# Expert rows of a fused attention and mixture-of-experts kernel: TensorE transposes replaced by DMA transposes of fp16 halves

## The chip, the cores and the metric

The kernel runs on one core of a Trainium2 chip. The metric is the device time of one execution in microseconds (us); lower is better. Names used below: PE is TensorE's matmul, PEld its weight load, DVE is VectorE, ACT is ScalarE, POOL is GpSimd, SP is the sync engine, which here only starts DMAs.

## The reference

Input x is 8 sequences of 512 tokens with 256 features, fp32: 4096 tokens. Each token is normalised (xn). Two branches read xn.

- A recurrent branch: q = xn Wq, v = xn Wv, a scan along the sequence (state = lam * state + v, one lam for each of 16 heads), y = q * state, layer norm of y with gain and bias, times silu(xn Wg), times Wo.
- A mixture of 8 experts, 2 for each token, with softmax gates of the two largest router logits. Its core is

```
def expert_step(acc, ew):
    wi, wo, g = ew
    h = x @ wi.T                      # 256 -> 2 x 512
    a, b = jnp.split(h, 2, axis=-1)
    o = jax.nn.silu(a) * b @ wo.T     # 512 -> 256
    return (acc + g[:, None] * o, None)
```

The output is x + s * silu(moe + bias), where s is the first branch.

## The kernel before, in words

All matmuls use fp16 operands with a high and a low half: a product is the sum of three matmuls (high by high, high by low, low by high), which the helper `three` issues (L1091).

First part, up to about 158 us: normalisation, routing, the recurrent branch chunk by chunk (8 chunks of 512 tokens), conversion of the expert weights to fp16 halves, and the sorting of tokens by expert. The sorting is done by GpSimd with 64 indirect DMAs (L462) that write each normalised row with four more columns (expert, two gate values, token number) to `slots_dram`, 260 words a row.

Second part, the expert blocks. 32 pair blocks (`PAIRS`) of 256 rows and 7 single blocks (`SINGLES`) of 128 rows. Block b uses buffer b % 2 of each kind. For a block:

- SP loads its rows from `slots_dram` to `slot_in` (`load_slots`, L346 to L353; the register with the row number is read with a small load from SBUF first). It waits until the buffer's last transposes are done (`slot_t_ps`) and until GpSimd has read the four extra columns of block b - 2 (`meta_ready`).
- PE transposes the fp32 rows to PSUM (`transpose_slots`, L1215: 4 instructions for a pair block, 2 for a single one), ACT copies them to fp16 (`high_slots`, L672), DVE writes the low half (`low_slots`, L995). Both land in `xT`, the moving operand of the first matmuls.
- PE computes `hidden(b, 0)` in bankA and `hidden(b, 1)` in bankB (24 matmuls each), ACT and DVE make silu(a) * b and its fp16 halves (L680, L1001, L685, L1005), and PE computes `outputs(b - 1)` in bankC (24 matmuls). The order on PE in the loop is hidden(b, 0), transposes of b + 1, hidden(b, 1), outputs(b - 1).
- DVE scales the result by the gate (L1020, `gate_y`), and GpSimd adds the rows to `y_dram` with two indirect DMAs (L532, `scatter_y`), each block after the scatters of the block before have landed. Then it works on the four extra columns of the next block (`meta`, L486 to L498, whose last instruction raises `meta_ready`).

Single blocks run with the roles of the operands exchanged (`row_hidden`, `transpose_g`). While early blocks run, SP also loads x for the last stage (L365, blocks 2 to 8) and the extra columns of the single blocks (L370, behind block 9).

Third part: `y_dram` comes back, silu, product with s, sum with x, store.

The order of work on each engine is written out by hand. Semaphores alone tie the engines together.

Of the kernel before, what the change touches and what calls it, by code (L numbers as in the profile page):

```python
# [33 lines left out]
P = 128  # L34
# [54 lines left out]
def scatters_before(b, i):  # L89

    if not isinstance(b, int):
        return b if i == 0 else b - 1
    return sum(units(a) for a in range(i, b, 2))

# [8 lines left out]
def build(nc, x, wq, wv, wg, wo, beta, ln_g, ln_b, router, w_exp, bias, out):  # L103
    ctx = ExitStack()
    with ctx:
# [52 lines left out]
        slot_in = [part(rows_raw, SB * ROW).rearrange("p (s r) -> p s r", r=ROW) for _ in range(2)]  # L158
# [83 lines left out]
        slots_ps = [bankD[:, i, :].rearrange("p (k n) -> p k n", k=KD) for i in range(2)]  # L242
# [9 lines left out]

        first_slots_ps = [bankB[:, i, :].rearrange("p (k n) -> p k n", k=KD) for i in range(2)]

        def slots_ps_of(b, i):
            return first_slots_ps[i] if isinstance(b, int) and b < 2 else slots_ps[i]

# [25 lines left out]
        slot_t_ps, slot_hi_ready, slot_lo_ready, h_ps, y_ps, y_sb = map(  # L283
            sem, ("slot_t_ps", "slot_hi_ready", "slot_lo_ready", "h_ps", "y_ps", "y_sb"))
# [21 lines left out]
        def _(sp):  # L306
# [39 lines left out]
            def load_slots(b, i):  # L346
                if not isinstance(b, int) or b >= 2:
                    sp.wait_ge(slot_t_ps, b - 1)
                if not isinstance(b, int) or 2 <= b < PAIRS + 2:
                    sp.wait_ge(meta_ready, b - 1)  # L350
                row = sp.value_load(blk_row[0:1, bass.ds(b, 1)], min_val=0, max_val=E * REGION // P)
                sp.dma_start(slot_in[i][:, 0:units(b), :], slots_v[:, bass.ds(row, units(b)), :])\
                  .then_inc(slot_loaded[i], 16)  # L353

            def two(b):
                load_slots(b, 0)
                load_slots(b + 1, 1)
# [14 lines left out]
            repeat(sp, X_EARLY + 3, PAIRS, 2, two)  # L372
            for b in range(PAIRS, BLOCKS):
                load_slots(b, b % 2)
# [5 lines left out]
            for i in range(2):  # L380
                sp.wait_ge(y_scattered[i], 16 * scatters_before(BLOCKS, i))
# [14 lines left out]
        def _(pool):  # L396
# [83 lines left out]
            def meta(b, i, first):  # L480

                pool.wait_ge(slot_loaded[i], b * 8 + 16 if i == 0 else b * 8 + 8)
# [3 lines left out]
                pool.tensor_tensor(is_first[i][:, :], slot_in[i][:, :, D], e_b, ALU.subtract)\  # L486
# [7 lines left out]
                pool.tensor_tensor(gate_c[i][:, :], slot_in[i][:, :, D + 1], is_first[i][:, :], ALU.mult)\  # L494
                    .then_inc(pool_step, 1)
                pool.wait_ge(pool_step, b * 3 + n_meta + 3)
                pool.tensor_tensor(gate_c[i][:, :], gate_c[i][:, :], slot_in[i][:, :, D + 2], ALU.add)
                pool.tensor_copy(dest_f[i][:, :], slot_in[i][:, :, D + 3]).then_inc(meta_ready, 1)  # L498
# [15 lines left out]
            def scatter_y(b, i, first=False):  # L514
# [7 lines left out]
                if not ones:  # L522
                    pool.wait_ge(meta_ready, b + 1)
                    if not isinstance(b, int) or b >= 2:
                        pool.wait_ge(y_scattered[i], 16 * scatters_before(b, i))
# [34 lines left out]
        def _(act):  # L560
# [78 lines left out]
            def recur(c, convert=True, last=False):  # L639
# [10 lines left out]
                if last:  # L650
                    act.wait_ge(rows_scattered, 16 * N_SCATTERS)
                    high_slots(0, 0, True)
                    high_slots(1, 1, True)
# [11 lines left out]
            def high_slots(b, i, first):  # L665
                act.wait_ge(slot_t_ps, b + 1)
                if isinstance(b, int) and b >= PAIRS + 2:
                    act.wait_ge(one_h_ps, b - PAIRS - 1)
                elif not first:
                    act.wait_ge(h_ps, b * 2 - 2)  # L670
                n = units(b) * P
                act.activation(xT[i][:, 0:KD, 0:n], slots_ps_of(b, i)[:, :, 0:n], ACT.Copy)\  # L672
# [15 lines left out]
            def halves(b, i, before, last=False):  # L688
                half(b, i, 0, before)
                if not last:  # L690
                    high_slots(b + 1, 1 - i, before == 0)
# [8 lines left out]
            split_p(CH)  # L700
            half(1, 1, 0, 1)
            keep_s(CH)
            high_slots(2, 0, False)
# [7 lines left out]
            for n in range(SINGLES):  # L711
# [7 lines left out]
                if n < SINGLES - 1:  # L719
                    high_slots(b + 1, 1 - i, False)  # L720
# [15 lines left out]
        def _(dve):  # L736
# [255 lines left out]
            def low_slots(b, i):  # L992
                dve.wait_ge(slot_hi_ready, b + 1)
                n = units(b) * P
                dve.tensor_tensor(xT[i][:, KD:2 * KD, 0:n], slots_ps_of(b, i)[:, :, 0:n],  # L995
                                  xT[i][:, 0:KD, 0:n], ALU.subtract).then_inc(slot_lo_ready, 1)
# [11 lines left out]
            def gate_y(b, i, first):  # L1008
# [6 lines left out]
                if not first:  # L1015

                    dve.wait_ge(y_scattered[i], 16 * scatters_before(b, i))
# [6 lines left out]
            def halves(b, i, last=False):  # L1024
                half(b, i, 0)
                if not last:
                    low_slots(b + 1, 1 - i)
# [7 lines left out]
            low_p(CH)  # L1035
            halves(1, 1)
# [10 lines left out]
            for n in range(SINGLES):  # L1047
# [6 lines left out]
                if n < SINGLES - 1:  # L1054
                    low_slots(b + 1, 1 - i)
# [30 lines left out]
        def _(pe):  # L1086
# [122 lines left out]
            def transpose_slots(b, i, first):  # L1209
                pe.wait_ge(slot_loaded[i], b * 8 + 16 if i == 0 else b * 8 + 8)  # L1210
                if not first:
                    pe.wait_ge(slot_lo_ready, b - 1)
                for k in range(KD):
                    for s in range(units(b)):
                        last = pe.transpose(slots_ps_of(b, i)[:, k, s * P:s * P + P],  # L1215
# [138 lines left out]
```

## Time and profile before

| | us |
|---|---|
| median of 3 runs | 508.69 (508.16 to 510.36) |
| the profiled execution, its own time | 510.48 |
| its span (first to last instruction) | 508.7 |
| PE busy | 425.2 (84%) |
| DVE busy | 304.3 (60%) |
| POOL busy | 275.1 (54%) |
| ACT busy | 214.3 (42%) |

The span is what the profiler recorded between the first and the last instruction; the execution's own time is 1.8 us longer. A share of busy time is an average over three parts with different limits, so the rows below are taken stage by stage.

### The profile page before, as it was taken

How to read it: one execution, taken by the hardware profiler on the slowest of the kernel's cores; microseconds unless marked ns; L12 is line 12 of the kernel's file. 1: busy time of each engine (PE TensorE's matmuls, PEld its weight loads, DVE VectorE, ACT ScalarE, POOL GpSimd, SP SyncE). 2: the span in 40 equal slices, each digit the busy share in tenths (PEclk: the TensorE clock that was granted, in tenths of full speed). 3: DMA queues.
4: the chain of work that ended last, by engine and by line, in shares of the span. 5: the costliest groups of instructions: out<-in, count | busy, mean ns of one | idle time of the engine just before them, and what ended most of it. 6: DMA issues, size and time to landing. Idle time of an engine off the chain costs nothing.

```text
span 508.7 us, 12049 instructions
## 1 busy us (share of the span) xinstructions
PE 425.2 (84%) x3446; PEld 337.6 (66%) x3447; DVE 304.3 (60%) x602; ACT 214.3 (42%) x340; POOL 275.1 (54%) x504
## 2 busy tenths in 40 slices
PE   1758784998898899999999989999999999998000
PEld 1544452565557798887898878888888888765000
DVE  4898899999965545454454544454545454444055
ACT  4882372778756534342324233333333333232041
POOL 4626786688772046564646474556565646543232
PEclk9999898999999999999999999999999999999755
DMA  8992275566933226455343433343334333342499
GB/s 250 290 362 94 84 244 190 164 240 242 329 121 84 82 46 144 106 101 104 54 73 52 73 53 50 64 67 62 58 66 69 61 56 59 65 64 32 73 310 349
DMA packets 52692, 64.70 MB, mean 127 GB/s; under 512 B 5552, under 2 KB 47536, under 8 KB 52656
## 3 DMA queue, kind: packets, MB, share of 16 engines
q1 hardware_dynamic: 37712, 45.55, 28.9%
q0 software_dynamic: 13296, 17.83, 20.8%
q10 hardware_dynamic: 1664, 1.06, 0.7%
q8 instruction: 10, 0.16, 0.1%
q14 instruction: 10, 0.08, 0.0%
HBM read 40.02 MB, written 28.74 MB: 135 GB/s over the span
## 4 chain that ended last, share of the span: by engine, by line
PE 40%; DMA 18%; issue 14%; DVE 13%; POOL 8%; ACT 3%; SPq 2%; DVEq 1%; POOLq 0%; ACTq 0%
PE bankC L1091 14%; PE bankB L1091 12%; DMA y_dram<-rows_raw 11%; PE bankA L1091 9%; POOL slots_dram L462 4%; DMA rows_raw<-slots_dram 4%; PE bankD L1215 2%; DMA w_raw<-x_in 2%; DVE rows_raw L1020 2%; POOL stat L426 1%; DVE w_raw L935 1%; DVE work L926 1%; DMA w_raw<-y_dram 1%; POOL y_dram L532 1%; DVE bn L751 1%
## 5 line engine op out<-in xcount | busy, mean ns | idle before, releaser
L532 POOL DMA_INDIRECT y_dram<-rows_raw x71 | 113.2, 1595 | 49.3 <-issue 31.0
L1091 PE MATMUL bankC<-w_raw,rows_raw 128*128 x852 | 99.5, 273 | 1.7 <-DVE rows_raw L1058 1.6
L1091 PEld LDWEIGHTS bankC<-w_raw,rows_raw 128*128 128x128 f16 x852 | 82.1, 98 | 13.3 <-issue 2.5
L462 POOL DMA_INDIRECT slots_dram<-rows_raw,pos_i x64 | 74.1, 1157 | 30.8 <-issue 20.0
L1091 PE MATMUL bankA<-rows_raw,w_raw 128*128 128x256 f16 x768 | 89.1, 273 | 1.2 <-DVE rows_raw L995 1.2
L1091 PE MATMUL bankB<-rows_raw,w_raw 128*128 128x256 f16 x768 | 89.1, 273 | 0.0
L1091 PEld LDWEIGHTS bankA<-rows_raw,w_raw 128*128 x768 | 75.0, 98 | 10.1 <-issue 1.4
L1091 PEld LDWEIGHTS bankB<-rows_raw,w_raw 128*128 x768 | 75.1, 98 | 8.3
L1005 DVE TENSOR_TENSOR rows_raw<-rows_raw 128x512 f16<-128x512 f32 x64 | 44.3, 692 | 45.7 <-ACT rows_raw L685 45.7
L1001 DVE SCALAR_TENSOR_TENSOR rows_raw<-rows_raw,bankA 128x512 f32<-128x512 f32 x32 | 22.0, 687 | 73.6 <-ACT rows_raw L680 73.6
L680 ACT ACTIVATE rows_raw<-bankA 128x512 f32<-128x512 f32 x32 | 19.1, 597 | 101.1 <-PE bankA L1091 101.1
L685 ACT ACTIVATE rows_raw<-rows_raw 128x512 f16<-128x512 f32 x64 | 40.3, 630 | 49.6 <-DVE rows_raw L1001 49.6
L526 POOL TENSOR_TENSOR spare<-spare 128x1 f32<-128x1 f32 x32 | 6.2, 192 | 95.7 <-DVE rows_raw L1020 94.7
L1020 DVE TENSOR_SCALAR rows_raw<-bankC,rows_raw 128x256 f32<-128x256 f32 x71 | 31.4, 480 | 9.6 <-DMA y_dram<-rows_raw 7.5
L1001 DVE SCALAR_TENSOR_TENSOR rows_raw<-rows_raw,bankB 128x512 f32<-128x512 f32 x32 | 22.0, 687 | 15.9 <-ACT rows_raw L680 15.9
L680 ACT ACTIVATE rows_raw<-bankB 128x512 f32<-128x512 f32 x32 | 19.1, 597 | 22.3 <-PE bankB L1091 22.3
L935 DVE SCALAR_TENSOR_TENSOR w_raw<-work,w_raw 128x1024 f32 (+1 forms) x24 | 27.7, 1215 | 0.0
L995 DVE TENSOR_TENSOR rows_raw<-bankD,rows_raw 128x512 f16<-128x512 f32 (+1 forms) x37 | 23.4, 633 | 2.4 <-ACT rows_raw L672 2.4
L1215 PE MATMUL bankD<-ident,rows_raw 128*128 128x128 f32 x134 | 21.4, 278 | 3.6 <-DMA rows_raw<-slots_dram 3.3
L426 POOL TENSOR_TENSOR stat<-stat,neg_half 128x4 f32<-128x4 f32 x16 | 16.9, 1058 | 13.0 <-DVE stat L964 12.2
L486 POOL TENSOR_TENSOR rows_raw<-rows_raw,blk_e 128x2 f32<-128x2 f32 x32 | 23.8, 743 | 0.0
L1091 PE MATMUL bankC<-wat_hi,work 128*128 128x256 f16 x128 | 22.3, 273 | 1.8 <-DVE work L980 1.4
(190 smaller groups left out, 641.2 us busy)
## 6 DMA issues: line engine op xcount, KB each, us to landing
work<-w_exp_in SPq DMA_DIRECT2D x24, 512.0 KB, 5.2
rows_raw<-slots_dram SPq DMA_DIRECT2D x32, 260.0 KB, 2.8
w_raw<-x_in SPq DMA_DIRECT2D x9, 512.0 KB, 4.4
y_dram<-bias_in SPq DMA_DIRECT2D x4, 1024.0 KB, 12.5
w_raw<-y_dram SPq DMA_DIRECT2D x8, 512.0 KB, 7.7
out<-w_raw SPq DMA_DIRECT2D x8, 512.0 KB, 5.7
work<-x_in SPq DMA_DIRECT2D x7, 512.0 KB, 4.4
slots_dram<-fill SPq DMA_DIRECT2D x9, 260.0 KB, 5.2
```

The costliest lines, as they stand in the source:

```text
L462: pool.indirect_dma_start(out=slots_dram, out_offset=bass.IndirectOffsetOnAxis(slot, 0), in_=row, in_offset=None, bounds_check=SLOTS - 1, ...
L486: pool.tensor_tensor(is_first[i][:, :], slot_in[i][:, :, D], e_b, ALU.subtract)\
L532: pool.indirect_dma_start(out=y_dram, out_offset=bass.IndirectOffsetOnAxis(to, 0), in_=ys[i][:, s, :], in_offset=None, bounds_check=ROWS_O ...
L680: act.activation(sil[j][:, :, 0:n], AB[j][:, :, 0:n], ACT.Silu, scale=1.0 / WSCALE).then_inc(sil_ready, 1)
L685: act.activation(g_hi[i][:, 2 * j:2 * j + 2, 0:n], g32[j][:, :, 0:n], ACT.Copy)\
L935: dve.scalar_tensor_tensor(w_lo[:, piece], wst[:, i % STAGES, :], WSCALE, w_hi[:, piece], ALU.mult, ALU.subtract).then_inc(w_lo_ready, 1)
L995: dve.tensor_tensor(xT[i][:, KD:2 * KD, 0:n], slots_ps_of(b, i)[:, :, 0:n], xT[i][:, 0:KD, 0:n], ALU.subtract).then_inc(slot_lo_ready, 1)
L1001: dve.scalar_tensor_tensor(g32[j][:, :, 0:n], sil[j][:, :, 0:n], 1.0 / WSCALE, AB[j][:, :, BLOCK:BLOCK + n], ALU.mult, ALU.mult).then_inc( ...
L1005: dve.tensor_tensor(g_lo[i][:, 2 * j:2 * j + 2, 0:n], g32[j][:, :, 0:n], g_hi[i][:, 2 * j:2 * j + 2, 0:n], ALU.subtract).then_inc(g_split, 1)
L1020: last = dve.tensor_scalar(ys[i][:, s, :], bankC[:, i, s * D:s * D + D], gates[:, s:s + 1], None, ALU.mult)
L1091: last = pe.matmul(out_ap, lhsT, rhs, start=(n == 0), stop=(n == len(todo) - 1))
L1215: last = pe.transpose(slots_ps_of(b, i)[:, k, s * P:s * P + P], slot_in[i][:, s, k * P:k * P + P], ident32[:, :])
```

## The change

- The rows of a block are loaded without the four extra columns (256 words instead of 260) to `slot_in`. The four columns are loaded by a DMA of their own to `meta_in` (`load_meta`), for the 32 pair blocks.
- ACT casts the rows to fp16 from SBUF, in the row layout, to the high half of `split16`, and DVE writes the low half beside it. The transposes on PE are gone. SP transposes the 128 x 512 fp16 values of each 128 rows with one DMA from SBUF to SBUF (`dma_start_transpose`), two for a pair block, one for a single block, 71 in all.
- ACT and DVE do this for block b + 2 between the two halves of block b (before: for block b + 1).
- SP's order for a block: load the extra columns of b (waits for `meta_ready` of b - 2); wait for `slot_lo_ready` of b and for both hidden halves of b - 2; load the rows of b + 2; transpose block b.
- PE waits for `xt_loaded` ahead of hidden(b, 0).

The core of the diff:

```diff
@@ SP @@
             def load_slots(b, i):
-                if not isinstance(b, int) or b >= 2:
-                    sp.wait_ge(slot_t_ps, b - 1)
-                if not isinstance(b, int) or 2 <= b < PAIRS + 2:
-                    sp.wait_ge(meta_ready, b - 1)
                 row = sp.value_load(blk_row[0:1, bass.ds(b, 1)], min_val=0, max_val=E * REGION // P)
-                sp.dma_start(slot_in[i][:, 0:units(b), :], slots_v[:, bass.ds(row, units(b)), :])\
+                sp.dma_start(slot_in[i][:, 0:units(b), :], slots_v[:, bass.ds(row, units(b)), 0:D])\
                   .then_inc(slot_loaded[i], 16)
+            def load_meta(b, i):
+                if not isinstance(b, int) or b >= 2:
+                    sp.wait_ge(meta_ready, b - 1)
+                row = sp.value_load(blk_row[0:1, bass.ds(b, 1)], min_val=0, max_val=E * REGION // P)
+                sp.dma_start(meta_in[i], slots_v[:, bass.ds(row, SB), D:ROW]).then_inc(meta_loaded[i], 16)
+            def transpose_slots(b, i):
+                sp.wait_ge(slot_lo_ready, b + 1)
+                if isinstance(b, int) and b >= PAIRS + 2:
+                    sp.wait_ge(one_h_ps, b - PAIRS - 1)
+                elif not isinstance(b, int) or b >= 2:
+                    sp.wait_ge(h_ps, b * 2 - 2)
+                if not isinstance(b, int) or b + 2 < BLOCKS:
+                    load_slots(b + 2, i)
+                for s in range(units(b)):
+                    sp.dma_start_transpose(xT[i][:, :, s * P:s * P + P],
+                                           split16[i][:, s, :, :].rearrange("p h d -> p (h d)"))\
+                      .then_inc(xt_loaded[i], 16)
+            for b in range(2):
+                load_slots(b, b)
+            for b in range(2):
+                load_meta(b, b)
+            for b in range(2):
+                transpose_slots(b, b)
...
@@ GpSimd, meta(b, i, first) @@
-                pool.wait_ge(slot_loaded[i], b * 8 + 16 if i == 0 else b * 8 + 8)
+                pool.wait_ge(meta_loaded[i], b * 8 + 16 if i == 0 else b * 8 + 8)
...
@@ ACT @@
-            def high_slots(b, i, first):
-                act.wait_ge(slot_t_ps, b + 1)
...
-                act.activation(xT[i][:, 0:KD, 0:n], slots_ps_of(b, i)[:, :, 0:n], ACT.Copy)\
+            def high_slots(b, i):
+                act.wait_ge(slot_loaded[i], b * 8 + 16 if i == 0 else b * 8 + 8)
+                if not isinstance(b, int) or b >= 2:
+                    act.wait_ge(xt_loaded[i], 16 * units_before(b, i))
+                act.activation(split16[i][:, 0:units(b), 0, :], slot_in[i][:, 0:units(b), :], ACT.Copy)\
                    .then_inc(slot_hi_ready, 1)
...
@@ DVE, low_slots(b, i) @@
-                dve.tensor_tensor(xT[i][:, KD:2 * KD, 0:n], slots_ps_of(b, i)[:, :, 0:n],
-                                  xT[i][:, 0:KD, 0:n], ALU.subtract).then_inc(slot_lo_ready, 1)
+                dve.tensor_tensor(split16[i][:, 0:units(b), 1, :], slot_in[i][:, 0:units(b), :],
+                                  split16[i][:, 0:units(b), 0, :], ALU.subtract).then_inc(slot_lo_ready, 1)
...
@@ PE @@
-            def transpose_slots(b, i, first):
-                pe.wait_ge(slot_loaded[i], b * 8 + 16 if i == 0 else b * 8 + 8)
...
+            def slots_here(b, i):
+                pe.wait_ge(xt_loaded[i], 16 * units_upto(b, i))
...
                 off = weights_at(b)
-                pe.wait_ge(slot_lo_ready, b + 1)
+                slots_here(b, i)
                 hidden(b, i, 0, off, False)
-                if not last:
-                    transpose_slots(b + 1, 1 - i, False)
                 hidden(b, i, 1, off, False)
                 outputs(b - 1, 1 - i, weights_at(b - 1), False)
```

Three places show how the rows of each engine's program move. First, PE in the pair loop, from the end of hidden(b, 0) in bankA to the start of hidden(b, 1) in bankB. Before (L1215 are the transposes of block b + 1):

```order
L1091 MATMUL bankA<-rows_raw,w_raw 128x256
L1210 ISA
L1215 MATMUL bankD<-ident,rows_raw 128x128 [waits slot_lo_ready,slot_loaded1]
L1215 MATMUL bankD<-ident,rows_raw 128x128 x3
L1091 ISA [waits g_ready]
L1091 MATMUL bankB<-rows_raw,w_raw 128x256 x2
```

The same place in the changed kernel:

```order
L1123 ISA
L1123 MATMUL bankA<-rows_raw,w_raw 128x256
L1123 ISA [waits g_ready]
L1123 MATMUL bankB<-rows_raw,w_raw 128x256 x2
L1123 ISA
```

The four transposes are gone from between the two halves. Second, PE at the head of a block in the loop (the load is of the block's weight offset). Before:

```order
L1207 TENSOR_LOAD blk_off
L1207 ISA x2
L1251 REGISTER_ALU
L1221 ISA [waits slot_lo_ready]
L1091 ISA [waits g_ready]
L1091 MATMUL bankA<-rows_raw,w_raw 128x256 x2
```

In the changed kernel:

```order
L1239 TENSOR_LOAD blk_off
L1239 ISA x2
L1242 ISA
L1246 ISA [waits xt_loaded0]
L1123 ISA [waits g_ready]
L1123 MATMUL bankA<-rows_raw,w_raw 128x256 x2
L1123 ISA
```

Ahead of hidden(b, 0) the wait is now for DMAs, where it was for DVE's `slot_lo_ready`. Third, SP for one pair block in its loop. Before (L351 is the load of the row number, L352 the DMA):

```order
L351 ISA [waits meta_ready,slot_t_ps]
L351 TENSOR_LOAD blk_row
L351 ISA x2
L352 ISA
L352 DMA rows_raw<-slots_dram 128x2x260
```

The same block in the changed kernel (L359 the extra columns, L352 the rows two blocks ahead, L370 the transposes):

```order
L358 ISA [waits meta_ready]
L358 TENSOR_LOAD blk_row
L358 ISA x2
L359 ISA
L359 DMA rows_raw<-slots_dram 128x2x4
L362 REGISTER_ALU
L366 ISA [waits slot_lo_ready]
L351 ISA [waits h_ps]
L351 TENSOR_LOAD blk_row
L351 ISA x2
L352 ISA
L352 DMA rows_raw<-slots_dram 128x2x256
L370 DMA_TRANSPOSE rows_raw<-rows_raw 128x4x128 x2
```

SP now issues four DMAs for a block instead of one, and the transposes stand behind two loads and three waits.

## Rows read from the trace of the kernel before

**Rows 1.** Page, part 4, the chain that ended last: shares of the span.

```profile
PE 40%; DMA 18%; issue 14%; DVE 13%; POOL 8%; ACT 3%; SPq 2%; DVEq 1%; POOLq 0%; ACTq 0%
```

**Rows 2.** Windows: stretch, length; busy us of PE, PEld, DVE, ACT, POOL; PEclk, DMA, GB/s.

```profile
174.20:432.00 257.80, 254.02 (x2302) 224.44 (x2301) 126.82 (x210) 89.13 (x152) 142.90 (x324) 1.00 0.42 74
```

**Rows 3.** Chain in order of time: start us, length us, what.

```profile
174.16 2.62 PE bankB L1091 x24
...
182.46 2.62 PE bankB L1091 x24
185.08 2.62 PE bankC L1091 x24
...
429.64 2.62 PE bankB L1091 x24
```

**Rows 4.** One line of the kernel (L1215): its instructions, and what they waited for.

```profile
L1215 PE MATMUL bankD<-ident,rows_raw x134: 272/273/332, 173.6 to 461.9; 128*128 128x128 f32 x134
...
  DMA rows_raw<-slots_dram: 10.4, 18
```

**Rows 5.** Timeline, one block: start us, length us, engine, line, instruction, [idle before].

```profile
331.29 2.78 PE L1091 MATMUL bankC<-w_raw,rows_raw 128*128 x24
...
332.85 0.19 POOL L498 COPY rows_raw<-rows_raw 128x2 f32<-128x2 f32 x1
333.91 2.78 PE L1091 MATMUL bankA<-rows_raw,w_raw 128*128 128x256 f16 x24
333.92 17.28 SPq L352 DMA_DIRECT2D rows_raw<-slots_dram  x3
...
335.17 0.19 POOL L526 TENSOR_TENSOR spare<-spare 128x1 f32<-128x1 f32 x1 [2.13 <-DVE rows_raw L1020]
...
340.92 0.19 POOL L498 COPY rows_raw<-rows_raw 128x2 f32<-128x2 f32 x1
```

**Rows 6.** DMA issues and queues: count, KB each, us to landing; packets, MB, share.

```profile
q1 hardware_dynamic: 37712, 45.55, 28.9%
q0 software_dynamic: 13296, 17.83, 20.8%
q10 hardware_dynamic: 1664, 1.06, 0.7%
...
rows_raw<-slots_dram SPq DMA_DIRECT2D x32, 260.0 KB, 2.8
...
rows_raw<-slots_dram SPq DMA_DIRECT2D x7, 130.0 KB, 2.1
```

**Rows 7.** Timeline of SP: seven loads in a row, no wait between.

```profile
231.06 7.39 SPq L370 DMA_DIRECT2D rows_raw<-slots_dram  x7
```

**Rows 8.** Timeline, start of the expert blocks.

```profile
153.97 8.80 SPq L352 DMA_DIRECT2D rows_raw<-slots_dram  x4
...
157.41 0.16 DVE L964 TENSOR_SCALAR stat<-mv 128x4 f32<-128x4 f32 x1
...
158.42 1.04 PE L1215 MATMUL bankB<-ident,rows_raw 128*128 128x128 f32 x8
...
160.64 2.79 PE L1091 MATMUL bankA<-rows_raw,w_raw 128*128 128x256 f16 x24 [1.19 <-DVE rows_raw L995]
```

**Rows 9.** Groups of instructions, 280 to 440 us: count, busy us, mean ns.

```profile
L685 ACT ACTIVATE rows_raw<-rows_raw 128x512 f16<-128x512 f32 x37 | 23.3, 630 | 28.5 <-DVE rows_raw L1001 28.5
...
L672 ACT ACTIVATE rows_raw<-bankD 128x512 f16<-128x512 f32 x17 | 9.9, 580 | 0.0
```

**Rows 10.** Timeline of PE in the first part, its longest idle time.

```profile
87.38 1.96 PE L1190 MATMUL bankD<-ident,work 128*128 128x128 f32 x8 [7.48 <-DVE work L939]
```

**Rows 11.** Windows, behind that idle time.

```profile
90.00:91.00 1.00, 1.00 (x4) 0.45 (x3) 1.00 (x4) 1.00 (x3) 0.00 (x0) 0.50 0.68 279
```

**Rows 12.** Timeline, scatters of two single blocks.

```profile
455.81 1.55 POOL L532 DMA_INDIRECT y_dram<-rows_raw  x1 [3.10 <-DVE rows_raw L1020]
...
460.42 1.55 POOL L532 DMA_INDIRECT y_dram<-rows_raw  x1 [3.06 <-DVE rows_raw L1020]
```

More of the change, by code:

```diff
@@ L93, in scatters_before, with units_upto @@
     return sum(units(a) for a in range(i, b, 2))
+def units_upto(b, i):
+    if not isinstance(b, int):
+        return b + 2 if i == 0 else b + 1
+    return sum(units(a) for a in range(i, b + 1, 2))
 def scatters_other(b, i):
@@ L371, in two @@
                           .then_inc(one_meta_loaded, 16)
-            repeat(sp, X_EARLY + 3, PAIRS, 2, two)
-            for b in range(PAIRS, BLOCKS):
-                load_slots(b, b % 2)
+            for b in range(2, X_EARLY + 3, 2):
+                two(b)
+            with sp.Fori(X_EARLY + 3, PAIRS - 3, 2) as b:
+                two(b)
+            for b in range(PAIRS - 2, BLOCKS):
+                next_slots(b, b % 2)
             sp.wait_ge(y_ps, BLOCKS)
@@ L686, in half, with halves @@
                    .then_inc(g_hi_ready, 1)
-            def halves(b, i, before, last=False):
+            def halves(b, i, before):
                 half(b, i, 0, before)
-                if not last:
-                    high_slots(b + 1, 1 - i, before == 0)
+                if not isinstance(b, int) or b + 2 < BLOCKS:
+                    high_slots(b + 2, i)
                 half(b, i, 1, before)
@@ L1022, in gate_y, with halves @@
                 last.then_inc(y_sb, 1)
-            def halves(b, i, last=False):
+            def halves(b, i):
                 half(b, i, 0)
-                if not last:
-                    low_slots(b + 1, 1 - i)
+                if not isinstance(b, int) or b + 2 < BLOCKS:
+                    low_slots(b + 2, i)
                 half(b, i, 1)
@@ L1035, in _ @@
             low_p(CH)
+            low_slots(2, 0)
             halves(1, 1)
@@ L1207, in weights_at @@
                 return pe.value_load(blk_off[0:1, bass.ds(b, 1)], min_val=0, max_val=(E - 1) * EW)
-            def transpose_slots(b, i, first):
-                pe.wait_ge(slot_loaded[i], b * 8 + 16 if i == 0 else b * 8 + 8)
[L1211 to L1215, printed above, removed]
-                                            slot_in[i][:, s, k * P:k * P + P], ident32[:, :])
-                last.then_inc(slot_t_ps, 1)
+            def slots_here(b, i):
+                pe.wait_ge(xt_loaded[i], 16 * units_upto(b, i))
             def hidden(b, i, j, off, first):
```

76 lines of the change are left out of this document (34 added, 42 removed).

## The prediction

> **What bounds the kernel now.** I read the chain of waits first, because it says which engine's work sets the end. TensorE (PE) has 40% of it [rows 1], more than twice any other. The windows view then says where: between 174.2 and 432.0 us, the pair blocks, PE is busy for 254.0 of 257.8 us at a granted clock of 1.00, the upper of its two levels, while DVE has 126.8, ACT 89.1 and POOL 142.9 us [rows 2]. So half of the execution is a loop bound by PE.
>
> The chain in order of time gives the period of that loop. hidden(b, 1), the bankB group, starts at 174.16 for block 1 and at 429.64 for block 31: 255.48 us for 30 blocks, 8.516 us a block. One group of 24 matmuls takes 2.62 us, and a block has three: 7.86 us [rows 3]. The other 0.656 us has two parts. Where nothing waits the period is 182.46 - 174.16 = 8.30 us, so the four transposes cost 0.44 us of PE a block, though each shows as 273 ns, because matmuls overlap. The remaining 0.216 us a block is PE waiting until rows have landed; the line of the transposes shows 18 such waits, 10.4 us (counted for matmul and weight load) [rows 4].
>
> Then the timeline of one block, for the chain that decides when rows come. outputs(b - 2) ends at 331.29 + 2.62 = 333.91. POOL starts its scatters at 335.17, and `meta` of block b, behind them, ends at 340.92 + 0.19 = 341.11, 7.2 us after the outputs. SP issues a load 0.88 us after such an end (333.04 to 333.92) [rows 5]. In the time that it waits for nothing SP needs (7.39 - 0.34) / 6 = 1.17 us for each load with its row number: seven of them take 7.39 us from first issue to end of the last, whose own issue takes some 0.34 us (an estimate from that group: 7 equal steps of 1.17 would be 8.2, less the reading of a row number that comes ahead of the first issue) [rows 7].
>
> Last, the tail: single blocks are paced by scatters that follow each other at 460.42 - 455.81 = 4.61 us [rows 12], and not by PE.
>
> **The change part by part.** PE loses 134 + 8 transposes. In the pair loop this is worth at most 30 x 0.656 = 19.7 us, if the waits for rows go too. Block 2's transposes, just before the 174.16 group, give 0.6 us more: by the neighbouring rows the group before them could end at 173.55. In the tail the saving is hidden behind the scatters: zero.
>
> ACT's cast from SBUF instead of PSUM costs 630 ns instead of 580 (a cast of the same size from SBUF stands beside it) [rows 9]; DVE's subtraction changes as little. Both engines have more than half of the loop free, so this costs nothing; without that cover it would be 0.05 us a block.
>
> The new term is the wait of PE for two DMA transposes. Nothing in this trace transposes by DMA. Call T the time that one takes in the DMA queues for 128 x 512 fp16, 128 KB. Bounds from the nearest rows: a plain load of 130 KB lands in 2.1 us and one of 260 KB in 2.8, so 0.7 us is the price of 128 KB moved as whole rows, on a fixed 1.4 [rows 6]. That is the low end. If the DMA goes in pieces of 128 elements, as the 128 x 4 x 128 shape of the instruction suggests, there are 512 pieces, 32 for each of 16 DMA engines. The queues' packets took 34 ns (q10: 0.7% of 16 x 508.7 us over 1,664), 62 ns (q1) and 127 ns (q0, the accumulating and scattering ones) [rows 6], so T is 1.1, 2.0 or 4.1 us. The high end is 4.1. I take 1.5, between the two queues without accumulation, which the new queue resembles most.
>
> The Trainium skill has two rules here that pull apart. Its page "Advanced Engine Details and Errata", section X-Bar Transpose (TRN2), says that such DMAs are as fast as regular ones. This is the low end, T = 0.7, and the sum below would be 493. Its page "VectorE: DVE Perf Modes", section on the three transpose paths, has 1309 ns for a 128 x 128 one by DMA and 390 ns by TensorE, and advises TensorE where PSUM will do. Read as throughput that is an estimated T of 5.2 us and a time of some 610; read as latency of one small transfer it says little about T. No row here decides between them.
>
> What a T of 1.5 does in the loop: SP's program for block b + 2 is load the extra columns (gated by `meta` of b), wait for low halves and hidden of b, load rows of b + 4, transpose. The first wait ends last, so the row load goes out at 0.88 + 1.17 = 2.05 us behind `meta`. The transposes queue behind its data, 2.8 us, then take 2T. In the block of [rows 5], with `meta` ended at 333.04, they land at 337.9 + 2T. At a period of 7.86 us PE wants them at 333.91 + 7.86 = 341.8. So T up to 1.9 us is hidden, and with 1.5 there are 0.8 us to spare. Above 1.9 the excess is 2T - 3.8, but this loop goes through outputs and `meta` of two blocks earlier, so a block pays half: T - 1.9. Behind SP's waits stand only its own later loads; the extra columns of b, issued a period ahead of POOL's use and small, are covered by 2.1 us of landing against about 7 us.
>
> Three costs outside the steady loop. First, the start. Before, loads are issued from 153.97, PE transposes at 158.42, and hidden(0, 0) starts at 160.64 [rows 8]. Now row load 0 lands at 156.8, ACT casts until 157.4, DVE is free at 157.57 and subtracts until 158.3; SP has issued loads 0 and 1 and two loads of extra columns by 157.8, issues the row load of block 2 at 159.1 (reading the row number first), and its data and 2T bring block 0's operands at 159.1 + 2.8 + 3.0 = 165.0. PE, idle from 158.4, starts 4.4 us later than before, and everything of block 0 and of chunk 7's transposes stands behind it. Second, the clock. After 7.48 us of idleness PE's clock stood at 0.50, its lower level, and was still there at 90 to 91 us, about 3 us after work resumed [rows 10, 11]. An idle time of 6.6 us may do the same: 3 us at half clock lose 1.5. Third, SP's seven loads for the single blocks stand between the transposes of blocks 9 and 10: 7 x 1.17, then 2 x 1.17 for block 10's own, 10.6 us against a period of 7.86, so 2.7 us late and, less 0.8 of slack, 1.9 us of stall; I take 2.
>
> Sum against the profiled execution's 510.48 us: - 19.7 - 0.6 + 4.4 + 1.5 + 2.0 = - 12.4, 498.1. The profiled execution is 1.8 us over the median of the runs shown, 508.69, so the median should come to 496.3; I say 496.
>
> **The rivals.** The same sum as a function of T is 496 + 30 x (T - 1.9, where positive) + 4 x (T - 1.5), the last for the start and the list of loads.
>
> Rival 1, slower: the DMA transposes are queue-bound. The place is the wait ahead of hidden(b, 0) of every pair block; it decides from T = 2.2 us, where the sum is the old median. The price at T = 3 is 33 + 6, 535 us; at the high end of 4.1 it is 66 + 10, 572. For it: GpSimd's scatters run at the same time and their packets cost 127 ns, and DMA engines are already at 0.42 of their time [rows 2, 6]. Against it: 256 KB of extra traffic a block is no more than the load that lands in 2.8 us.
>
> Rival 2, a smaller gain: T is near 1.5, but the transposes hold up the scatters. In the tail each scatter is on the path; 0.7 us on each of nine would be 6 us, 502. For it: the tail has nothing else to wait for. Against: each single block has one transpose in 4.61 us.
>
> Rival 3, no change: T between 2.1 and 2.35, or a start and an early part (where 512 KB loads of x stand in the same queue ahead of transposes) that cost 10 us more than summed: 506 to 511. Here the edit would not do what it says, since PE's freed time comes back as a wait for the same queue.
>
> **How the numbers follow.** Forecast, T up to 1.9: 0.50, 489 to 500. Rival 2: 0.10. Rival 3: 0.10. Rival 1: 0.30. A change of 0.5% is about what a measurement of this kernel can tell from none, 506.1 to 511.2: faster 0.60, same 0.09, slower 0.31. Likeliest 496. The range starts at 489 (T = 0.7 gives 493, less the clock's 1.5 and the list's 2) and reaches to 530, T of 2.8; most of rival 1 beyond that is the part left out. The likeliest case alone is 489 to 500.
>
> **What would show it.** Period of the bankB groups 7.86 us with no wait for DMA in blocks 11 to 31; DMA transposes landing within about 5 us of issue; one idle time of PE of 6 to 7 us before hidden(0, 0) and a clock of 0.50 behind it; one stall of about 2 us before hidden(10, 0); single blocks still 4.6 us apart. The prediction is wrong if PE waits for `xt_loaded` in most blocks; then T is over 1.9 us and half the excess should show in the period.

## The result

| | before | changed |
|---|---|---|
| median of 5 runs each, same chip, us | 509.41 (508.16 to 510.36) | 505.93 (504.86 to 507.31) |
| the profiled execution, its own time | 510.48 | 507.31 |
| its span | 508.7 | 505.5 |

The ratio is 0.993, 95% interval 0.9912 to 0.9949: faster by 3.5 us, 0.7%. A ratio with its interval is computed from the single executions, without those in a slower state that every kernel shows now and then, so it can differ a little from the quotient of two medians. The forecast was 496, faster by 12.4. The direction is right, the size less than a third. The time lies inside the stated range of 489 to 530, but only because that range was made wide for transposes that are slow in the queues, which is not what happened; it lies outside the 489 to 500 of the likeliest case.

### The profile page after: what moved, and what is told of

Read it like the earlier page. It is cut to its first block, busy times and chain, and to the rows that moved or that the text cites. A ratio compares the mean times of both kernels' runs of the same rounds, so it can differ in the third digit from the quotient of the medians.

```text
span 505.5 us, 11980 instructions
## 1 busy us (share of the span) xinstructions
PE 411.5 (81%) x3304; PEld 324.7 (64%) x3305; DVE 300.3 (59%) x602; ACT 215.1 (43%) x340; POOL 281.4 (56%) x504
## 2 busy tenths in 40 slices
DMA packets 100021, 74.01 MB, mean 146 GB/s; under 512 B 52880, under 2 KB 94864, under 8 KB 99984
## 3 DMA queue, kind: packets, MB, share of 16 engines
q1 hardware_dynamic: 85040, 54.86, 41.2%
## 4 chain that ended last, share of the span: by engine, by line
PE 39%; DMA 17%; DVE 15%; issue 13%; POOL 8%; SPq 5%; ACT 2%; DVEq 0%; POOLq 0%; ACTq 0%
PE bankC L1123 13%; PE bankA L1123 13%; PE bankB L1123 12%; DMA y_dram<-rows_raw 11%; POOL slots_dram L496 4%; DMA rows_raw<-rows_raw 3%; DMA w_raw<-x_in 2%; POOL stat L460 1%; SPq L370 1%; DVE w_raw L967 1%; DVE work L958 1%; DVE rows_raw L1051 1%; DMA w_raw<-y_dram 1%; DVE bn L984 1%; DVE bn L783 1%
## 5 line engine op out<-in xcount | busy, mean ns | idle before, releaser
L1123 PE MATMUL bankA<-rows_raw,w_raw 128*128 128x256 f16 x768 | 92.4, 279 | 14.1 <-DMA rows_raw<-rows_raw 14.1
L1123 PEld LDWEIGHTS bankA<-rows_raw,w_raw 128*128 x768 | 76.2, 100 | 25.9 <-issue 15.6
L520 POOL TENSOR_TENSOR rows_raw<-rows_raw,blk_e 128x2 f32<-128x2 f32 x32 | 27.2, 850 | 0.0
L1026 DVE TENSOR_TENSOR rows_raw<-rows_raw 128x512 f16<-128x512 f32 (+1 forms) x39 | 24.9, 638 | 2.4 <-ACT rows_raw L703 2.4
L692 ACT ACTIVATE work<-bankD,stat 128x256 f32<-128x256 f32 x32 | 15.4, 563 | 19.2 <-POOL stat L461 19.2
L664 ACT ACTIVATE w_raw<-work 128x1024 f32 (+1 forms) x24 | 23.4, 1045 | 0.2 <-DMA work<-w_exp_in 0.2
L703 ACT ACTIVATE rows_raw<-rows_raw 128x512 f16<-128x512 f32 (+1 forms) x39 | 22.5, 577 | 1.6 <-DMA rows_raw<-slots_dram 1.6
```

The source lines that it names most:

```text
L520: pool.tensor_tensor(is_first[i][:, :], meta_in[i][:, :, 0], e_b, ALU.subtract)\
L664: act.activation(w_hi[:, bass.ds((c * PIECES + i) * PIECE, PIECE)], wst[:, i % STAGES, :], ACT.Copy, scale=WSCALE).then_inc(w_hi_ready, 1)
L703: act.activation(split16[i][:, 0:units(b), 0, :], slot_in[i][:, 0:units(b), :], ACT.Copy)\
L1026: dve.tensor_tensor(split16[i][:, 0:units(b), 1, :], slot_in[i][:, 0:units(b), :], split16[i][:, 0:units(b), 0, :], ALU.subtract).then_inc ...
L1123: last = pe.matmul(out_ap, lhsT, rhs, start=(n == 0), stop=(n == len(todo) - 1))
```

## The profile after

The chain of waits of the changed kernel in order of time (start us, length us, what), the lines that answer to [rows 3]: hidden(b, 1) of block 1, of two blocks of the steady loop with what stands between them, and of block 31.

```profile
177.50 2.62 PE bankB L1123 x24
...
315.30 2.62 PE bankB L1123 x24
317.92 2.62 PE bankC L1123 x24
320.54 2.62 PE bankA L1123 x24
323.15 2.62 PE bankB L1123 x24
...
425.34 2.62 PE bankB L1123 x24
```

A block takes 323.15 - 315.30 = 7.85 us, three groups of 2.62 with nothing between (7.86 with rounding). From 315.30 to 425.34 it is 110.04 us for 14 blocks, 7.86 each. But the whole stretch from block 1 to block 31 takes 247.84 us, and 30 x 7.86 is 235.8: 12.0 us are lost, the last of them at block 17.

The waits of PE for the transposes, which stand in the place of [rows 4]: first the line of the waits view (us in total, times, longest), then the timeline's lines of two of the five, with the idle time ahead of the group in brackets.

```profile
PE bankA L1123 <- DMA rows_raw<-rows_raw: 14.1, 5, 5.8
```

```profile
163.01 4.20 PE L1123 MATMUL bankA<-rows_raw,w_raw 128*128 128x256 f16 x24 [4.78 <-DMA rows_raw<-rows_raw]
...
254.21 4.67 PE L1123 MATMUL bankA<-rows_raw,w_raw 128*128 128x256 f16 x24 [5.82 <-DMA rows_raw<-rows_raw]
```

These are the start and block 10. Behind these two idle times the group takes 4.20 and 4.67 us, where it takes 2.62 in the chain and 2.79 in this view when nothing slows it. The other three waits are before blocks 5, 9 and 17 (1.33, 0.94 and 1.22 us). The first group answers to the last of [rows 8] and starts 2.4 us later.

SP's timeline around block 10's wait, with the seven loads of [rows 7]:

```profile
235.07 0.37 SPq L352 DMA_DIRECT2D rows_raw<-slots_dram  x1
235.49 2.55 SPq L370 DMA_TRANSPOSE rows_raw<-rows_raw  x2
238.08 0.58 SPq L396 DMA_DIRECT2D work<-x_in  x1
239.44 7.23 SPq L401 DMA_DIRECT2D rows_raw<-slots_dram  x7
247.88 0.38 SPq L359 DMA_DIRECT2D rows_raw<-slots_dram  x1
249.40 0.39 SPq L352 DMA_DIRECT2D rows_raw<-slots_dram  x1
249.83 2.79 SPq L370 DMA_TRANSPOSE rows_raw<-rows_raw  x2
```

Here is what the prediction had nowhere: two DMA transposes keep SP itself for 2.55 us, where the issue of a plain load is 0.37. The line of the transposes, over all 71 (ns, minimum, median, maximum of one issue):

```profile
L370 SPq DMA_TRANSPOSE rows_raw<-rows_raw x71: 1189/1229/2315, 159.0 to 455.0; - x71
```

The chain shows when they land, counted from the beginning of the issue of a block's second transpose: for block 10 it is 2.52 us, for block 17, with a scatter issued at 307.86 beside it, 4.07. Block 10 is not the usual case. The completion events of the trace give the same time for all 32 pair blocks: 2.4 to 4.7 us, 3.55 in the median.

```profile
251.42 2.52 DMA rows_raw<-rows_raw
254.21 4.67 PE bankA L1123 x24
...
306.94 1.23 SPq L370
308.21 4.07 DMA rows_raw<-rows_raw
```

The windows view, as in [rows 2] (stretch, length, busy time of PE, PEld, DVE, ACT, POOL, clock, DMA share, GB/s). In the last stretch PE is busy in 108.78 of 110 us, and the DMA engines in 0.63 of the time, against 0.42 in the pair blocks before. In the first and third the clock is below 1.00, its mean over the stretch: these hold the two long waits.

```profile
158.00:174.00 16.00, 10.55 (x83) 8.53 (x80) 5.34 (x9) 8.19 (x15) 3.05 (x14) 0.89 0.31 67
174.00:251.00 77.00, 71.42 (x648) 62.91 (x648) 38.13 (x66) 27.80 (x47) 41.82 (x91) 1.00 0.75 131
251.00:308.00 57.00, 53.79 (x476) 47.51 (x477) 25.20 (x43) 18.75 (x32) 31.91 (x69) 0.94 0.58 93
308.00:418.00 110.00, 108.78 (x998) 97.16 (x996) 56.53 (x97) 40.83 (x70) 68.83 (x154) 1.00 0.63 100
```

A short stretch inside block 10's slow group shows the clock itself, 0.50 of full speed:

```profile
255.00:257.00 2.00, 2.00 (x12) 1.41 (x10) 0.00 (x0) 0.00 (x0) 1.28 (x7) 0.50 0.80 69
```

The page's queues (packets, MB, share), to be held against [rows 6]: q1 has 85,040 packets instead of 37,712, q0 and q10 have as many as before.

```profile
q1 hardware_dynamic: 85040, 54.86, 41.2%
q0 software_dynamic: 13296, 17.83, 21.3%
```

The scatters of single blocks on POOL, answering to [rows 12]:

```profile
456.56 1.55 POOL L566 DMA_INDIRECT y_dram<-rows_raw  x1 [2.97 <-DVE rows_raw L1051]
461.22 1.55 POOL L566 DMA_INDIRECT y_dram<-rows_raw  x1 [3.11 <-DVE rows_raw L1051]
466.76 1.55 POOL L566 DMA_INDIRECT y_dram<-rows_raw  x1 [3.99 <-DVE rows_raw L1051]
```

The steps are 4.66 and, once, 5.54 us. The balance of the two spans:

| stretch | before | changed | difference |
|---|---|---|---|
| up to block 1's bankB group | 174.16 | 177.50 | +3.34 |
| from there to block 31's | 255.48 | 247.84 | -7.64 |
| from there to the end of the span | 79.06 | 80.16 | +1.10 |
| span | 508.7 | 505.5 | -3.2 |

The middle was to give 17.7 (19.7 less 2.0 for the seven loads). It gave 7.64.

## Experiments

The theory: SP's time. Each DMA transpose costs SP 1.23 us, which the forecast had at nothing, so the seven loads (7.23 us), an x load and the transposes' own issue add up to a wait of 5.8 us before block 10, and the small reserve of the other blocks is gone whenever a scatter is late. The first rival: the queues are full (DMA share 0.75 between 174 and 251 us), and the transposes wait for other traffic. All ratios are to the kernel before, on the same chip.

### e1_spread: the seven loads apart

```diff
-                if isinstance(b, int) and b == X_EARLY + 1:
-                    for n in range(SINGLES):
...
+                if isinstance(b, int) and b >= X_EARLY + 3:
+                    n = (b - X_EARLY - 3) // 2
...
-            for b in range(2, X_EARLY + 3, 2):
+            for b in range(2, X_EARLY + 3 + 2 * SINGLES, 2):
```

> The changed kernel with SP's seven small loads for the single blocks (one_in) spread, one behind each pair of blocks 10 to 22, instead of all seven behind block 9. Theory (SP's own time): those loads and the 1.23 us that SP needs to issue each DMA transpose put the transposes of block 10 late; the stall of PE before hidden(10, 0), 5.8 us idle and 2.05 us lost to the lower clock behind it, goes, and the time falls by 7 to 8 us against the changed kernel's 505.9, to about 498. Rival (contention of DMA traffic in the early blocks, the loads of x and the scatters): PE waits there all the same, and the time stays within 2 us of 505.9.

Measured: 501.23 us (500.51 to 502.0), ratio 0.9835 (0.9813 to 0.9856), 4.7 us under the changed kernel (4.8 by the ratios). That is less than the 7 to 8 us that were expected, and more than the 2 us that the rival allowed. The 5.82 us before block 10 are gone, and no group of the pair blocks behind block 1 runs at the lower clock. From block 1 to block 31 it is 419.09 - 177.90 = 241.19 us, 5.4 over the 235.8: the 7.87 us of block 10 went and the short waits grew by 1.2, together 6.65. The medians show less of it because the profiled execution of the changed kernel is the slowest of its five. Five short waits stay, 0.5 to 1.2 us each, such as this:

```profile
199.49 2.79 PE L1123 MATMUL bankA<-rows_raw,w_raw 128*128 128x256 f16 x24 [0.63 <-DMA rows_raw<-rows_raw]
```

The same seven loads, with the same bytes, are in the same queue; only SP's order is another. Full queues don't explain the long wait before block 10, whose transposes landed in 2.52 us. They may have a share in the short ones: the transposes ahead of this kernel's five short waits landed 3.6 to 5.3 us after their issue.

### e2_first: transposes ahead of the loads

```diff
@@ SP, transpose_slots(b, i) @@
-                if not isinstance(b, int) or b + 2 < BLOCKS:
-                    load_slots(b + 2, i)
+                row = sp.value_load(...)
                 for s in range(units(b)):
                     sp.dma_start_transpose(...)
+                if more:
+                    sp.dma_start(slot_in[i]..., slots_v[row]...)
@@ next_slots @@
+                transpose_slots(b, i)
                 if not isinstance(b, int) or b < PAIRS:
                     load_meta(b, i)
-                transpose_slots(b, i)
```

> The changed kernel with SP's order for a block turned: the transposes of block b come first (behind the waits for its low halves and for hidden of b - 2, with the reading of the row number ahead of them), then the row load of b + 2, then the load of the extra columns with its wait for GpSimd. In the changed kernel the transposes are issued 2.7 us behind GpSimd's last meta instruction; here they need not wait for it, and go out 2 to 3 us sooner. Theory (what is late is their issue on SP): the small stalls before blocks 5, 9 and 17 (4.0 us together) go, and the one before block 10 shrinks from 7.9 to 1 or 2 us: about 496. Rival (the transposes themselves are slow in the queue, over 1.9 us each): waits of PE stay in most of the places where they are, under 3 us are gained: 503 or more.

Measured: 499.5 us (497.06 to 501.16), ratio 0.979 (0.9761 to 0.9819). That lies between the theory's 496 and the rival's 503: the short waits are gone as the theory has it, but the long one cost 4.2 us, not 1 or 2.

```profile
248.20 4.46 PE L1127 MATMUL bankA<-rows_raw,w_raw 128*128 128x256 f16 x24 [2.39 <-DMA rows_raw<-rows_raw]
```

From block 1 to block 31: 417.71 - 177.69 = 240.02, 4.2 over 235.8, which are the 2.39 of idleness and 4.46 - 2.62 = 1.84 at the lower clock. Two things were moved at once here (the row load and the load of the extra columns, both behind the transposes), so the run doesn't say which of the two gave more. The order changed one thing besides SP's waiting: the transposes now go out before the scatters instead of beside them, and land in 2.5 us in the median, where it was 3.55 (completion events, 32 pair blocks each). No run separates the two effects.

### e3_both: the two edits together

> Both edits: the seven loads spread and the transposes first. Theory: no wait of PE for transposes is left from block 2 on, every period is 7.86 us, 30 blocks take 235.8 us where the changed kernel needs 247.8: 12 us less, 494. Rival (contention): PE still waits in blocks 2 to 9, and 497 to 500 results.

Measured: 493.95 us, ratio 0.9705 (0.9673 to 0.9737). The chain, hidden(b, 1) of blocks 1 and 31, and the only wait for a transpose that is left, the start (4.29 us idle):

```profile
161.20 4.26 PE bankA L1127 x24
...
175.75 2.62 PE bankB L1127 x24
...
411.55 2.62 PE bankB L1127 x24
```

411.55 - 175.75 = 235.80 us, 30 times 7.86: the pair loop has no wait. SP's list and SP's order together account for all of the 12.0 us. (PE came free 1.3 us earlier at the end of the first part in this execution than in the profiled one of the changed kernel, so stretches are compared, not start times.) The same kernel once more:

> The kernel of e3_both once more, on the same chip as e5_start's and the one with extra transposes in the tail. Expected from its first measurement: a ratio to before of 0.9705 (0.967 to 0.974), some 494 us, with no wait of PE for DMA from block 2 to block 31 and 30 blocks in 235.8 us. The stretch from block 31's bankB group to the end of the span is 80 to 81 us.

Measured: 494.75 us, ratio 0.9707 (0.9674 to 0.9739), the same. The stretch behind block 31's bankB group is 491.5 - 411.50 = 80.0 us.

### e4_extra: two more transposes a block

e1_spread, and from block 10 to block 31 SP issues two more DMA transposes, of constants into a buffer that nothing reads, ahead of the real ones.

```diff
+                for s in range(2 if extra else 0):
+                    sp.dma_start_transpose(scratch[s], wat_hi[:, s, ...]).then_inc(extra_done, 16)
                 for s in range(units(b)):
                     sp.dma_start_transpose(xT...)
```

> The kernel with the seven loads spread, and in blocks 10 to 31 two more DMA transposes of constants to a scratch buffer, issued just ahead of the two real ones. Theory (each costs SP 1.23 us of issue and no more; the DMA engines have room): the real ones land 2.5 us later; 0.65 us of slack is used up, and the rest, 1.8 us, is halved because the chain from outputs to the transposes spans two blocks: a period of about 8.8 us and 20 us more than the kernel with the loads spread. Rival (queue-bound, 2 us or more for each in the DMA engines): 4 us or more later, the period over 9.6 us and 38 us more.

Measured: 518.14 us (516.74 to 519.9), ratio 1.0208 (1.0172 to 1.0244). The ratio is 0.0373 over that of e1_spread, some 19 us, where SP's time asked for 20 and full queues for 38. Two bankA groups that are 16 blocks apart:

```profile
266.75 2.81 PE L1133 MATMUL bankA<-rows_raw,w_raw 128*128 128x256 f16 x24 [1.08 <-DMA rows_raw<-rows_raw]
...
406.22 2.79 PE L1133 MATMUL bankA<-rows_raw,w_raw 128*128 128x256 f16 x24 [0.19 <-issue]
```

139.47 / 16 = 8.72 us a block. SP's timeline over three of its blocks (L376 the added transposes, L380 the real ones, L362 the extra columns, L355 the rows, L411 one of the seven loads):

```profile
329.63 2.54 SPq L376 DMA_TRANSPOSE wat_lo<-wat_hi  x2
332.22 2.67 SPq L380 DMA_TRANSPOSE rows_raw<-rows_raw  x2
336.04 0.39 SPq L362 DMA_DIRECT2D rows_raw<-slots_dram  x1
337.26 0.37 SPq L355 DMA_DIRECT2D rows_raw<-slots_dram  x1
337.68 2.52 SPq L376 DMA_TRANSPOSE wat_lo<-wat_hi  x2
340.24 2.68 SPq L380 DMA_TRANSPOSE rows_raw<-rows_raw  x2
344.04 0.36 SPq L411 DMA_DIRECT2D rows_raw<-slots_dram  x1
...
346.82 2.52 SPq L376 DMA_TRANSPOSE wat_lo<-wat_hi  x2
```

From one block's transposes to the next it is 8.05 us, and 9.14 with one of the seven loads between, 8.6 on average. Between 260 and 350 us SP waits for 3.0 us in all, so here its issuing is the bound. Behind block 22 the seven loads are through and the step is still 8.1 to 9.2 us; there SP also waits for `meta` (4.0 us between 350 and 440 us), so the loop through the scatters has its share. The added transposes also settle their size in the queues, from the pages of e1_spread and of this kernel, with spans of 499.2 and 516.0 us:

```profile
q1 hardware_dynamic: 85040, 54.86, 41.7%
```

```profile
q1 hardware_dynamic: 108976, 60.63, 45.8%
```

44 transposes add 23,936 packets, 544 each, and 0.458 x 16 x 516.0 - 0.417 x 16 x 499.2 = 450 us of engine time: 19 ns a packet, 0.64 us of all 16 engines for one transpose. This is T as the prediction defined it.

### e6_before_spread: the same list spread in the kernel before

> The kernel before, with the same seven loads spread, one behind each pair of blocks 10 to 22. It shows what the list of seven costs where one load a block is all that SP does. PE waits 0.83 us for rows before block 10's transposes there. Theory (SP's time became scarce only with the change): 0 to 1.5 us less than before, 508 to 509.4. Rival (the list was as costly before): 5 us or more less.

Measured: 507.23 us (505.48 to 509.12) against 507.87, ratio 0.9983 (0.9963 to 1.0002). In the kernel before, the list cost nothing that can be told from zero. It is the change that made it cost the 4.7 us of e1_spread.

### e5_start and e9_start_again: the first two blocks transposed by PE

e3_both, and blocks 0 and 1 as in the kernel before (fp32 transposes on PE to bankB, ACT's and DVE's halves from PSUM).

```diff
+                for b in range(2):
+                    pe.wait_ge(slot_loaded[b], 16)
...
+                            last = pe.transpose(first_slots_ps[b][...], slot_in[b][...], ident32[:, :])
+                    last.then_inc(slot_t_ps, 1)
```

> Both edits, and blocks 0 and 1 are transposed by PE as in the kernel before (in fp32 to bankB, split by ACT and DVE from there). Theory: the start of the expert blocks costs 3.9 us in the changed kernel (hidden(1, 1) begins at 177.5 where the kernel before without block 2's transposes would begin at 173.6), 4.8 us of idle PE and the lower clock behind it; both go: 3 to 4 us under the run with both edits, about 490. Rival (the lower clock and the idle time are made up for later, since the tail is paced by scatters): under 1.5 us.

> The kernel of e5_start once more, beside e3_both's. Theory: the first two blocks transposed by PE win 2.4 us at the start in every execution, so the median lies 2 to 3 us under e8_both_again's, unless the tail gives it back. Rival: the blocks, now 2.4 us earlier, meet the scatters at another phase and the tail lengthens by as much; then the median is within 1 us of e8_both_again's and the profiled tail is longer than 82 us.

Measured: 495.03 us (490.47 to 498.83), ratio 0.9655 (0.9618 to 0.9691), and 492.43 us (490.1 to 496.09), ratio 0.9653 (0.9616 to 0.969), 2.3 us under e8_both_again on the same chip. The first run expected 3 to 4 us and about 490; by the ratios it is 2.5 us under e3_both. The start is as the theory has it. The chain of e5_start:

```profile
160.25 2.79 PE bankA L1139 x24
...
173.33 2.62 PE bankB L1139 x24
```

The group is at the upper clock, and block 1's bankB starts 2.4 us earlier than e3_both's. But the profiled executions (495.26 and 496.09 us) give it back in the tail. e9_start_again's goes from 409.33 (block 31's bankB in the chain) to 494.3, 85.0 us, where e8_both_again has 411.50 to 491.5, 80.0. Most of the loss is older than the tail: POOL's scatters never came earlier with PE. POOL's first instruction for block 1's scatters, which waits for those of block 0, in e9_start_again and in e8_both_again:

```profile
190.64 0.19 POOL L568 TENSOR_TENSOR spare<-spare 128x1 f32<-128x1 f32 x1 [4.61 <-DMA y_dram<-rows_raw]
```

```profile
190.71 0.19 POOL L564 TENSOR_TENSOR spare<-spare 128x1 f32<-128x1 f32 x1 [2.48 <-DMA y_dram<-rows_raw]
```

PE is 2.2 us ahead, and POOL begins at the same time. From there on the scatters follow PE at a greater distance. Block 31's second scatter starts 430.59 - 409.33 = 21.26 us behind that block's bankB group, where it is 428.81 - 411.50 = 17.31 in e8_both_again: 4.0 of the 5.0 us. The rest is the step behind it:

```profile
430.59 1.56 POOL L574 DMA_INDIRECT y_dram<-rows_raw  x1 [0.30 <-issue]
436.28 1.55 POOL L574 DMA_INDIRECT y_dram<-rows_raw  x1 [4.13 <-DVE rows_raw L1067]
```

The step is 5.7 us. e8_both_again has 433.55 - 428.81 = 4.74 at that place. In both profiles of this kernel the scatter that comes first here is issued within half a microsecond of a DMA transpose; in e7_tail so is the one at 432.96, and the step behind it is 4.78, so that alone doesn't make a step long. Why block 0's scatters land later when PE starts earlier is not shown. Of what the second run expected, the theory has the median (2.3 us under) and the rival the profiled tail (over 82 us). The intervals of e8_both_again and e9_start_again overlap a little, and the executions of one kernel lie 6 to 9 us apart here. So the start's 2.4 us are shown in the trace, and how much of them reaches the median is not settled.

### e7_tail: do transposes hold up scatters?

e3_both with one more DMA transpose behind the row load of each single block.

```diff
+                if isinstance(b, int) and b >= PAIRS:
...
+                    sp.dma_start_transpose(scratch, wat_hi[:, 0, ...]).then_inc(extra_done, 16)
```

> e3_both with one more DMA transpose (of constants, into a buffer that nothing reads) behind the row load of each of the seven single blocks, where each scatter is on the path. Theory (rival 2 of the prediction holds): transposes in flight stretch the landing of scatters, so scatters of single blocks, 4.6 us apart before, are 5.0 us or more apart and the tail from block 31's bankB group to the end is 83 us or more, the median 3 us or more over e8_both_again's. Rival: scatters are not held up by transposes; they stay 4.6 us apart, the tail stays at 80 to 81 us, and the median within 1 us. SP has room for the extra issue: 1.17 + 3 x 0.4 + 2 x 1.23 is about 4.1 to 4.6 us a block with all its issues, just under the step of 4.6.

Measured: 495.23 us (493.56 to 497.98), ratio 0.971 (0.9681 to 0.974), 0.5 us over e8_both_again. The tail is 496.2 - 415.34 = 80.9 us. Both are as the rival has it. Four of its scatters:

```profile
437.74 1.55 POOL L577 DMA_INDIRECT y_dram<-rows_raw  x1 [3.23 <-DVE rows_raw L1062]
442.45 1.55 POOL L577 DMA_INDIRECT y_dram<-rows_raw  x1 [3.16 <-DVE rows_raw L1062]
...
451.53 1.55 POOL L577 DMA_INDIRECT y_dram<-rows_raw  x1 [3.01 <-DVE rows_raw L1062]
457.05 1.55 POOL L577 DMA_INDIRECT y_dram<-rows_raw  x1 [3.97 <-DVE rows_raw L1062]
```

From 437.74 to 451.53 there are three steps of 4.6 on average, then one of 5.52, as the changed kernel has one of 5.54. Twice the transposes don't make more long steps, so one more transpose a block doesn't hold up the scatters. The long step of the changed kernel (461.22 to 466.76) even has none beside it, since its last transpose is issued at 455.0. The kernel before has no step over 4.86 us in its tail. Where the long steps come from stays open, also the one of e9_start_again.

## Why the forecast was too large, step by step

**The loop gain, -19.7.** The mechanism was right: without the transposes a block takes 7.86 us, and blocks 17 to 31 run at that. The forecast had no wait in blocks 11 to 31; there is one, before block 17. Blocks 5, 9 and 17 lose 1.5, 1.1 and 1.4 us, 4.0 together, which the sum didn't have. The chain shows them behind late scatters (block 5's: a scatter that landed 5.55 us after its issue; block 17's: a scatter that POOL started 0.8 us later than usual, as it does at this place in the kernel before too). The transposes themselves also landed late there, 4.11, 3.39 and 4.07 us after their issue instead of 2.5, and with 2.5 next to nothing of these waits would be left. e2_first shows that SP's order let both through to PE; it took away SP's waiting and the late landings at once, so which of them weighed more stays open.

**T, 1.5, and the reserve of 0.8 us.** T is 0.64, near the low end of 0.7 and far from the high end of 4.1: the packets of a transpose take 19 ns, not the 34 to 127 of the rows used, and they are 544, near the 512 counted. What the Trainium skill states in "Advanced Engine Details and Errata", section X-Bar Transpose (TRN2), that such a DMA is as fast as a regular one, holds here for the queue's time (0.64 us against 0.7). The time of 493 that goes with it was missed all the same. The landing came out about as forecast, for another reason. In the steady loop `meta` ends at 327.81 and SP sends the transposes at 330.52:

```profile
327.62 0.19 POOL L532 COPY rows_raw<-rows_raw 128x2 f32<-128x2 f32 x1
```

```profile
330.52 2.54 SPq L370 DMA_TRANSPOSE rows_raw<-rows_raw  x2
```

The second one begins 1.27 us later, and lands 3.5 us after that, 7.5 us behind `meta`, where the forecast had 7.86. PE wants them at 336.26, 8.45 behind. So SP takes for issuing what the forecast gave to the queues, and about 1 us is to spare; with the 2.4 to 4.7 us over all pair blocks it is between 2 us and nothing.

**SP's seven loads, +2.0: the step that failed.** The prediction put 10.6 us between the transposes of blocks 9 and 10. It was 249.83 - 235.49 = 14.34 us. The missing 3.8 are 2.55 for the issue of block 9's own transposes, taken as nothing, and 239.44 - 238.08 = 1.36 for an x load with its register work, which stands at the same place (the loads themselves took 0.2 less than counted). The wait was 5.82 us instead of 1.9, and like the one at the start it had the lower clock behind it: 4.67 - 2.62 = 2.05 us more, which the prediction had for the start alone. Together 7.87 instead of 2.0. e1_spread took this away, e2_first made it 4.2 by its order, e6_before_spread showed that the list was harmless before. So the step that failed is the cost of issuing on SP: the prediction added up SP's loads at 1.17 us each and put the issue of a transpose, 1.23 us, at nothing.

**Start and clock, +4.4 + 1.5 - 0.6 = +5.3.** Measured +3.34. PE idled 4.78 us instead of 6.6 and hidden(0, 0) came 2.4 us later instead of 4.4, since SP sent the transposes right behind the row load and they landed 2.5 us later (160.34 to 162.88). They didn't wait for the 2.8 us of its data: in e3_both, with no row load ahead of them, the landing took 2.48 us, here 2.54. The lower clock cost 4.20 - 2.79 = 1.4 (a group behind a wait is 2.79 at the upper one), as forecast.

**Tail, 0.** +1.1, of which the one long scatter step is 0.9. Rival 2 had 6 us there from T on each of nine scatters; e7_tail speaks against it.

**ACT and DVE, nothing.** As said: a cast of a pair block takes 614 ns, and no group of PE waits for one. DVE waits for ACT's casts twice, 2.4 us together, off the chain.

The sum with measured terms: the loop gives 255.48 - 235.80 = 19.68, the waits take 12.04 back (7.9 at block 10, 4.0 at the other three, the rest in smaller pieces), the start 3.34 and the tail 1.10: - 3.2, the difference of the spans. Against the forecast's - 12.4 that is 9.2 us less: 5.9 at block 10, 4.2 at the other waits, 1.1 in the tail, less 2.0 that the start cost less than forecast. The miss would have been larger without this last error, which went the other way. Rival 1, queue-bound transposes, fell with T of 0.64; e4_extra, with 4 transposes a block, took 19 us more and not 38. (By the prediction's own formula T of 2.1 and 2.35 give 504.4 and 512.9, not the 506 and 511 of rival 3.) Rival 3's time is nearly the measured one, but its mechanism, the same queue, is not: PE's freed time came back as a wait for SP's issuing, which e3_both removed with as much traffic in the queues (100,021 packets in the one page, 100,023 in the other).

## What to carry to other kernels

A transfer has three prices: the issuing engine's time, the queues' time and the landing. Where work moves to DMAs, add up the issuing engine's program for one period and for its longest straight piece, with everything that already stands in it; a list that was free where the issuing engine had nothing else to do is not free once something urgent stands behind it. Then issue the urgent transfers first and spread the rest: here that turned a gain of 0.7% into one of 3%. With PE keeping the first two blocks 3.5% were measured, with intervals that overlap those of the 3%. And look at where the scatters are when PE gets faster: an engine that was off the path can keep the old time.

## What the hardware showed

- The issue of a DMA transpose of 128 x 512 fp16 from SBUF to SBUF kept SP for 1.19 us at least, 1.23 in the median and 2.32 at most, that of a plain load of rows for 0.33 to 0.40. It made 544 packets (19 ns each).
- A block's second transpose landed 2.4 to 4.7 us after its issue began in the changed kernel (median 3.55, scatters issued beside it) and in 2.5 us in the median in e3_both (scatters issued some 3 us later). That the scatters make the difference is not shown by an experiment.
- Idle times of PE of 2.39, 4.29, 4.78 and 5.82 us were each followed by a group of 4.46, 4.26, 4.20 and 4.67 us instead of 2.62, part of it at a granted clock of 0.50, the lower of the two levels, 1.2 GHz. In e4_extra one of 4.75 us was followed by 5.30. Behind idle times of 0.6 to 1.7 us the group took 2.79 to 2.81.
- Where PE waited for nothing, as in e3_both from block 1 to 31, 30 blocks took 235.80 us, 30 times the three groups.
